# Taking the cross attention's row statistics in the self attention stage of a decoder block

## The reference

```python
x = x + attn(layernorm(x))          # differential self attention, 16 heads, causal
x = x + xattn(layernorm(x), ctx)    # cross attention, 8 heads of 16 channels, rotary
x = x + ffn(layernorm(x))           # 32 experts, 6 per token, and a shared expert
def _layernorm(x, axis=-1, eps=1e-05):
    m = jnp.mean(x, axis=axis, keepdims=True)
    v = jnp.var(x, axis=axis, keepdims=True)
    return (x - m) / jnp.sqrt(v + eps)
```

## Time and profile before

| | |
|---|---|
| runs | 3850.41, 3853.70, 3856.12 us; median 3853.7 |
| the profiled execution | 3853.95 us, its span 3852.2 us |
| PE busy | 3673.2 us, 95% of the span |
| DVE busy | 2859.0 us, 74% |
| ACT busy | 2361.7 us, 61% |
| POOL busy | 1793.6 us, 47% |

### The profile page before, as it was taken

The page is one execution under the profiler, slowest core; times in us unless marked ns, Lnnn a source line. Parts: engine busy times, 40 slices in busy tenths (PEclk is TensorE's granted clock), DMA queues, the critical chain, the costliest instruction groups (busy, mean ns, idle before and its releaser), DMA issues.

```text
span 3852.2 us, 74126 instructions
## 1 busy us (share of the span) xinstructions
PE 3673.2 (95%) x24778; PEld 2904.3 (75%) x24778; DVE 2859.0 (74%) x5969; ACT 2361.7 (61%) x5418; POOL 1793.6 (47%) x2121
## 2 busy tenths in 40 slices
PE   7999999879999999999799999999999999999999
PEld 6888888644444444444589999999999999999998
DVE  5777777668888888888547777777777777777333
ACT  5777777647777777777525555555555555555221
POOL 2233323234555555555325566665665666655210
PEclk8999999879999999999899999999999999999999
DMA  5000000033344344444139999999999999998421
GB/s 207 24 24 23 29 24 21 18 102 117 125 128 128 125 132 131 125 152 151 41 101 267 267 266 266 265 266 267 265 266 264 265 264 265 267 267 240 153 86 60
DMA packets 290168, 621.37 MB, mean 161 GB/s; under 512 B 70000, under 2 KB 78576, under 8 KB 289664
## 3 DMA queue, kind: packets, MB, share of 16 engines
q1 hardware_dynamic: 224640, 464.01, 36.9%
q0 software_dynamic: 64000, 150.52, 16.1%
q10 hardware_dynamic: 1152, 2.10, 0.1%
HBM read 459.93 MB, written 155.98 MB: 160 GB/s over the span
## 4 chain that ended last, share of the span: by engine, by line
PE 79%; DVE 8%; ACT 8%; issue 3%; POOL 0%; DMA 0%; SPq 0%; DVEq 0%; ACTq 0%; POOLq 0%
PE ps L615 17%; PE ps L617 16%; PE ps L616 16%; PE ps L798 6%; PE ps L602 6%; ACT PA L1003 5%; PE ps L759 4%; PE ps L781 4%; PE ps L892 2%; PE ps L918 2%; PE ps L642 2%; DVE aw L1306 2%; PE ps L719 2%; ACT PX L1070 1%; DVE NM L1403 1%
## 5 line engine op out<-in xcount | busy, mean ns | idle before, releaser
L615 PE MATMUL ps<-WG,XT 128*128 128x352 f32 x2304 | 766.0, 332 | 7.9 <-DVE XT L1580 5.4
L616 PE MATMUL ps<-WG,XT 128*128 128x352 f32 x2304 | 744.6, 323 | 0.0
L617 PE MATMUL ps<-WG,XT 128*128 128x352 f32 x2304 | 744.4, 323 | 0.0
L1403 DVE TENSOR_REDUCE NM<-ps 128x2 f32<-128x1024 f32 x512 | 614.6, 1218 | 71.7 <-PE ps L759 67.4
L1070 ACT ACTIVATE PX<-ps 128x1024 f32<-128x1024 f32 x512 | 523.6, 1023 | 199.4 <-PE ps L781 183.9
L1897 POOL DMA_INDIRECT sum<-YO,TI x224 | 396.2, 1769 | 502.4 <-issue 396.3
L1216 ACT ACTIVATE HS<-ps 128x352 f32<-128x352 f32 x288 | 134.0, 465 | 564.9 <-PE ps L617 564.9
L1586 DVE TENSOR_TENSOR HS<-ps,HS 128x352 f32<-128x352 f32 x288 | 151.1, 525 | 428.9 <-ACT HS L1216 425.4
L1544 DVE TENSOR_TENSOR WG<-WL,WG 128x704 fp32r<-128x704 f32 x528 | 450.3, 883 | 23.6 <-ACT WG L1183 23.6
L615 PEld LDWEIGHTS ps<-WG,XT 128*128 128x128 f32 x2304 | 434.6, 189 | 9.1 <-DVE XT L1580 6.3
L616 PEld LDWEIGHTS ps<-WG,XT 128*128 128x128 f32 x2304 | 435.1, 189 | 0.0
(11 more groups left out here) (275 smaller groups left out, 8515.6 us busy)
## 6 DMA issues: line engine op xcount, KB each, us to landing
WL<-in_w_gate SPq DMA_DIRECT2D x128, 704.0 KB, 4.2
WL<-in_w_up SPq DMA_DIRECT2D x128, 704.0 KB, 5.9
DL<-in_w_down SPq DMA_DIRECT2D x128, 512.0 KB, 8.3
kq_parts<-HL SPq DMA_DIRECT2D x64, 512.0 KB, 3.1
KS<-kq_parts SPq DMA_DIRECT2D x384, 64.0 KB
QS<-kq_parts SPq DMA_DIRECT2D x384, 64.0 KB
DL<-in_w_down SPq DMA_DIRECT2D x128, 192.0 KB, 8.9
CB<-sum POOLq DMA_DIRECT2D x64, 256.0 KB, 3.0
```

The costliest lines, as they stand in the source:

```text
L615: pe.matmul(out_, lh(0), rh(0), start=first, stop=False)
L616: pe.matmul(out_, lh(0), rh(1), start=False, stop=False)
L617: return pe.matmul(out_, lh(1), rh(0), start=False, stop=last)
L1403: dve.tensor_reduce(NM[:, g % 2, qc, p:4:2], ps[:, 512 * bk:512 * bk + 1024].rearrange("p (i k) -> p i k", k=512), AX.X, ALU.max, negate=T ...
```

## The change

The statistics of the summed rows, which the cross attention's norm needs, are taken from `XA` right after the sum, not from the copy that comes back from DRAM. In `self_part` the step `stats_m(b-2)` stands between `add_x` and `store_x`. It leaves round 9 of the cross attention. `sX` has a pair for each of the 32 blocks, so POOL no longer waits for `norm_m` of the block before. `norm_m` on ACT now has a wait for the load of its rows, which `stats_m` on DVE had before. `load_x` on SP gets one more wait, for the statistics of the block that had the buffer of `XA`. `SG`, a small buffer, is placed over another one's space.

```diff
         if odd or late:
             do("add_x", b - 2)
+            do("stats_m", b - 2)
             do("store_x", b - 2)
         if odd:
             do("stats", b + 5)
...
         if 0 <= n < 16 * NB:
             do("top", n)
-        do("stats_m", b + 2)
...
-        sX = sb(ax, "sX", [128, 2])
+        sX = sb(ax, "sX", [128, NB, 2])
...
             def norm_m(b):
+                q, before = place_of(b)
                 act.wait_ge(S["l_nx"], 3 * b + 3)
+                act.wait_ge(S["d_x%d" % q], 16 * (XL[q] + before + 1))
                 if b:
                     act.wait_ge(S["p_r"], 4 * b)
-                act.activation(xm[:, :], XB[:, place_of(b)[0], :], ACT.Identity, bias=sX[:, 0:1], scale=sX[:, 1:2]
+                act.activation(xm[:, :], XB[:, q, :], ACT.Identity, bias=sX[:, b, 0:1], scale=sX[:, b, 1:2]
                                ).then_inc(S["a_nm"], 1)
...
+            def stats_m(b):
+                dve.wait_ge(S["v_x1"], b + 1)
+                if b:
+                    dve.wait_ge(S["l_nx"], 3 * b)
+                statistics(XA[:, b % NXA, :], 1, "v_nx", b)
...
-            def stats_m(b):
-                q, before = place_of(b)
-                dve.wait_ge(S["d_x%d" % q], 16 * (XL[q] + before + 1))
-                if b:
-                    dve.wait_ge(S["l_nx"], 3 * b)
-                statistics(XB[:, q, :], 1, "v_nx", b)
...
+                if name == "stats_m" and 0 <= n < NB:
+                    power(n, 1, sX[:, n, :], "v_nx", "l_nx")
...
-            def stats_m(b):
-                if b:
-                    pool.wait_ge(S["a_nm"], b)
-                power(b, 1, sX, "v_nx", "l_nx")
...
                 if b >= NXA:
                     sp.wait_ge(S["d_st%d" % ((b - NXA) % NXB)], 16 * ((b - NXA) // NXB + 1))
+                    sp.wait_ge(S["v_nx"], 2 * (b - NXA) + 1)
```

More of the change, by code:

```diff
@@ L496, in build @@
         GW = sb(ax, "GW", [128, 4, 32])
+        [SG] = place(SG=([128, 32],))
         LQ = sb(ax, "LQ", [128, 4, 16])
@@ L519, in build @@
         M = sb(ax, "M", [128, 32])
-        SG = sb(ax, "SG", [128, 32])
         SM = sb(ax, "SM", [128, 1])
@@ L1383, in self_step @@
                         {"tops": tops, "weigh": weigh, "scaled": scaled}[name](n)
-                elif name in ("stats", "norm_x", "evict_q", "evict_k", "mean_square", "norm_o", "add_x") and 0 <= n < NB:
+                elif name in ("stats", "norm_x", "evict_q", "evict_k", "mean_square", "norm_o", "add_x",
+                              "stats_m") and 0 <= n < NB:
                     if name == "norm_o" and n == 2:
@@ L1387, in self_step @@
                     {"stats": stats, "norm_x": norm_x, "evict_q": evict_q, "evict_k": evict_k,
-                     "mean_square": mean_square, "norm_o": norm_o, "add_x": add_x}[name](n)
+                     "mean_square": mean_square, "norm_o": norm_o, "add_x": add_x, "stats_m": stats_m}[name](n)
                     if name == "norm_x" and n == 1:
@@ L1521, in cross_step @@
             def cross_step(name, b, *at):
-                steps = {"top": top, "stats_m": stats_m, "stats_g": stats_g, "rotate": rotate, "sums": sums, "shares": shares,
+                steps = {"top": top, "stats_g": stats_g, "rotate": rotate, "sums": sums, "shares": shares,
                          "join": join, "gate": gate, "narrow": narrow, "choose": choose, "weights": weights, "rank": rank,
@@ L1831, in cross_step @@
             def cross_step(name, b, *at):
-                steps = {"stats_m": stats_m, "stats_g": stats_g, "total": total, "low": low, "spread": spread,
+                steps = {"stats_g": stats_g, "total": total, "low": low, "spread": spread,
                          "low_c": low_c, "low_m": low_m, "low_o": low_o, "rows": first_rows}
```

## The result

The changed kernel takes 3878.06 us (median of 5 runs, 3870.14 to 3882.41) beside 3854.1 us of the kernel before on the same chip. The ratio, which goes by all runs and not by the two medians, is 1.0058, with a 95% interval of 1.0042 to 1.0074 (16 to 29 us): slower, by 24 us between the medians where 13.5 were forecast, and outside the range of 3851 to 3875. The profiled execution of the changed kernel took 3880.35 us, its span is 3878.6 us, and the mean granted clock is 0.980 instead of 0.984.

A forecast was written before the change was run, and what follows sets the result against it. The self attention's loop through ACT, DVE and PE, closed by the exponentials, was taken to bound the kernel. 3853.95 + 13.7 - 0.2 = 3867.5 us; own range 3864 to 3873, range of 8 in 10 3851 to 3875.

The forecast's parts named there:

- The step of the self attention: End of odd half blocks: the added DVE statistics delay the maxima 0.86 us, the exponentials 0.57 us a block, 24 x 0.57 = 13.7 us.
- the spare time: Before the exponentials in the self attention's step: the maxima can come 0.29 us later without delaying them.
- the tie of the earlier trace: Where DVE splits weights, kernel before: `nb` starts at 139.29 together with POOL's subtraction and takes 1.32 us instead of 0.17.
- POOL: Self attention: three added small operations delay POOL's 128x512 subtraction, so `nb` starts ahead of it by 0.37 us.
- the rival: POOL gets the port first in the self attention: subtraction holds `nb`, 1.52 us a block, 36 us, 3890 us; chance 0.10.
- the weight splitting step: Self attention step where DVE splits the cross attention's weights: `nb` starts with the port free, 0.2 us won, once.
- The rule of the Trainium skill: Self attention: by it POOL's second power would hold `nb` another 0.17 us, 0.74 a block, 18 us in all.
- The cross attention: Statistics removed from DVE and POOL there: gain between nothing and 0.6 us plus 0.1 us a block; taken as nothing.
- The rival in which it gives back 26 us: Cross attention, queue over `shares` to PE's transposition: up to 0.82 us a block come back, 3841 us; chance 0.09.
- The stage doesn't feel it: Self attention: a queue of PE closes the loop or the maxima overlap more, price near zero, 3854 us; chance 0.16.
- the place where the stages meet: Between self attention and cross attention: 1 us each way allowed in the forecast's own range.
- The base: Whole kernel before: the profiled execution's 3853.95 us, 0.25 us above the median of the runs, to which the terms were added.

## Why the prediction was right or wrong

**The step of the self attention: right, term by term.** The new bn_stats starts 0.71 us behind the sum (0.72 forecast), the maxima 0.85 us later (0.86), a block is 0.57 us longer (0.57), and three kernels put the spare time at 0.28 to 0.32 us (0.29). The cross attention starts 14.8 us later in one profiled execution where 24 x 0.57 = 13.7 were worked out; between repeats that start moves by 3 us by itself, and the block with the tie of the earlier trace rows moves it most. This block was 23.4 us long in the trace of before and 24.6 in the changed one, 1.2 us more and not 0.57, at a granted clock of 1.00 and 0.93. That the sum came within 1.1 us is therefore partly luck.

**POOL: right, with a wider margin than I had.** `nb` is ahead of the subtraction by 0.51 us (0.37 forecast; the new three operations take 442.01 - 440.69 = 1.32 us and not 1.22), and because POOL is delayed by its own operations: without them the distance is zero. In the one step in which `nb` lost the tie it cost 1.1 us over the changed kernel's step (1.52 - 0.57 = 0.95 by the rival), and 3 us more at a lower clock, which the rival didn't have. In the weight splitting step `nb` and the subtraction of the changed kernel read

```profile
140.03 0.17 DVE L1274 TENSOR_SCALAR nb<-nm 128x8 f32<-128x8 f32 x1
```
```profile
140.55 1.29 POOL L1780 TENSOR_TENSOR oTL<-oT,OTH 128x512 fp32r<-128x512 f32 x1
```

so the collision of the earlier trace rows is gone there, too. (The forecast's 140.26 should have been 139.29 + 0.94 = 140.23.) The 0.2 us that I gave for it can't be seen: two of five traces of the same instructions have no collision there before the change either, and the clock moves this block by more. The power of 0.56 us from 442.32 on runs beside the `nb` at 442.57, which still takes 0.17 us, and a block costs 0.57 us and not 0.74. The rule of the Trainium skill (SBUF — State Buffer, section Who interferes with whom), by which VectorE in its two-port mode and GpSimd block each other for a whole instruction, is not what the trace shows for operations of this size. With the 128x512 subtraction it is: the second `nb`, at 444.10, takes 0.30 us and ends 0.03 us behind the subtraction.

**The cross attention: right.** I took nothing, between bounds of nothing and 0.6 us with 0.1 a block; it gave 1 us. The rival in which it gives back 26 us fell with the 0.81 us by which `shares` came forward and PE did not.

**The stage doesn't feel it: wrong as a rival.** It was given 0.16 because PE's records fill 94% of the stage. They filled 92% of it afterwards with the same matmuls: the share said nothing on whether PE had a queue. What did was PE's wait for the weights, 0.7 us in each half block, here in the kernel before over 200 to 680 us (total, times, longest):

```profile
PE ps L602 <- DVE aw L1306: 29.4, 43, 0.7
```

In the ten blocks of the forecast this wait is 13.7 us, and in those of the changed kernel 19.6.

**What failed is a term that the sum doesn't have: the clock at the cross attention's end.** For that place it was put at nothing without a reason. The sum goes from the self attention's 13.5 us straight to the end, as if all that follows were only shifted, with "1 us each way for the place where the stages meet". That place was looked at where the cross attention begins. Where it ends, 1086 to 1096 us pass from the first `NM` to the first `HS`, and in the changed kernel 7.0 us more than before, 5.1 of them in two stretches at a lower clock. The windows of the kernel before could have told that there is such a term: between 1830 and 1897 its granted clock is 0.87, 0.90 and 0.83, so PE goes part of the time at each of its two levels there. They could not have told its size. By the table of the experiments a shift can save 2 us or cost 9, so the term should have been -2 to +9 us, and the likeliest case's range 3862 to 3882.

**The base** was perhaps 2 to 3 us low: 3853.95 us against medians of 3856 to 3857 over 11 to 21 runs (3854.1 over the 5 beside the result). Together 3856.5 + 13.5 + 7 = 3877 us (the 7 already contain the 1 us that the cross attention gives back), where 3878 and 3879 were measured; the last 1 to 2 us are within what the runs of one kernel spread.

## What to carry to other kernels

Find the spare time of the one instruction that closes the loop, and count what is put ahead of it beyond that; the same two instructions cost some 13 us of the stage in front of the maxima and nothing 4 us later in the queue, where the engine waits anyway. Take a step from an engine only where somebody waits for what stands behind it. And where the profile shows TensorE between its two clocks, a shift of a few microseconds ahead of that place has a price of its own; a delay put in once, in front of it, and the granted clock of equal stretches behind it show that.

## What the runs showed of the hardware

- The same stretch of work at the cross attention's end (58 matmuls) took 11.0 us at a granted clock of 1.00, 12.3 to 12.4 at 0.86 and 14.5 to 14.9 at 0.65 to 0.66; another (78 matmuls) took 22.9 us at 0.85 and 25.4 to 25.5 at 0.64. Which it was changed with a delay far ahead of it.
- At 1.2 GHz eight matmuls of L798 took 1.93 us, at 2.4 GHz 1.06 us.
- On DVE an operation that needs the result of a 128x512 one starts 0.71 to 0.73 us behind its start, an independent one 0.60, and one behind a bn_aggr that it doesn't need 0.10.
- When `nb` on DVE and a 128x512 subtraction on POOL start within the same 10 ns, either can be the one that waits, and it differs between executions of the same instructions: in three of five `nb` took 1.32 us, in two the subtraction took 1.31 or 1.32 us and `nb` 0.17.
